# Attention of a layered kernel: turnings of two steps issued together, the value products of both behind them

## What is computed

```python
q = (hidden @ Wq.T).reshape(b, s, 32, 64);  k, v = ...  # 8 heads each, repeated 4 times
q, k = rope(q), rope(k)
logits = jnp.einsum('bhqd,bhkd->bhqk', q, k) / 8
attn = softmax(where(causal, logits, min))
out = jnp.einsum('bhqk,bhkd->bhqd', attn, v).reshape(b, s, 2048) @ Wo.T
x = x + out * silu(sign_layer(xn))
```

## Time and profile before

| | us |
|---|---|
| median of 3 runs | 779.48 (778.21 to 781.17) |
| the profiled execution, its own time | 780.78 |
| its span, first to last instruction | 779.0 |
| TensorE busy, of the span | 706.5 (91%) |
| VectorE, ScalarE, GpSimd busy | 477.7, 417.9, 399.3 |
| share of TensorE in the chain that ended last | 64% |

### The profile page before, as it was taken

How to read it: one execution, slowest core, us unless ns; L and a number is a source line. 1 busy time by engine, 2 the same in 40 slices (tenths; PEclk the granted TensorE clock), 3 DMA queues, 4 the chain that set the end, 5 groups by cost and what they waited for, 6 DMA issues and landing times.

```text
span 779.0 us, 13360 instructions
## 1 busy us (share of the span) xinstructions
PE 706.5 (91%) x4536; PEld 618.6 (79%) x4536; DVE 477.7 (61%) x1023; ACT 417.9 (54%) x1043; POOL 399.3 (51%) x451
## 2 busy tenths in 40 slices
PE   2999999999999991388889999999999999999995
PEld 2887989989989981266678888888888888888874
DVE  7582644423323445485566787777877778777764
ACT  4446244233233234236467776677766777667663
POOL 1412442332332220326777776787767877677460
PEclk9899999999999996599899999999999999999999
DMA  5075877778787505235224323322233222232001
GB/s 187 28 253 186 280 251 249 237 253 254 248 254 250 171 15 155 41 116 147 82 69 117 67 62 69 89 69 64 65 69 89 71 58 67 58 89 56 1 1 54
DMA packets 101859, 96.21 MB, mean 124 GB/s; under 512 B 50592, under 2 KB 72032, under 8 KB 101664
## 3 DMA queue, kind: packets, MB, share of 16 engines
q1 hardware_dynamic: 99584, 89.33, 39.6%
q0 software_dynamic: 2208, 6.03, 2.2%
HBM read 69.24 MB, written 9.31 MB: 101 GB/s over the span
## 4 chain that ended last, share of the span: by engine, by line
PE 64%; DVE 10%; POOL 9%; ACT 8%; issue 6%; SPq 1%; POOLq 1%; DMA 1%; DVEq 0%; ACTq 0%
PE bank L1631 15%; PE bank L1491 8%; PE bank L1665 8%; PE bank L1492 8%; PE bank L1493 8%; PE bank L1487 6%; POOL prob L1449 5%; ACT prob L1264 3%; PE bank L1752 3%; DVE nmax L1010 2%; PE bank L1753 2%; POOL q_lo L1461 2%; ACT kv_hi L1271 2%; DVE o_lo L1023 1%; POOL wq_lo L1429 1%
## 5 line engine op out<-in xcount | busy, mean ns | idle before, releaser
L1449 POOL TENSOR_TENSOR prob<-prob,rinv 128x128 f32<-128x128 f32 (+3 forms) x256 | 177.6, 724 | 102.1 <-DVE rinv L1015 102.1
L1264 ACT ACTIVATE prob<-bank,nmax 128x512 f32<-128x512 f32 (+3 forms) x256 | 133.2, 528 | 45.4 <-DVE nmax L1010 43.9
L1019 DVE TENSOR_TENSOR kv_lo<-bank,kv_hi 128x512 fp32r<-128x512 f32 x160 | 110.0, 687 | 52.7 <-ACT kv_hi L1271 51.8
L1271 ACT ACTIVATE kv_hi<-bank 128x512 fp32r<-128x512 f32 x160 | 96.3, 602 | 78.7 <-PE bank L1487 78.6
L1631 PEld LDWEIGHTS bank<-xgT,wm 128*128 128x128 f32 x920 | 108.1, 192 | 5.3 <-issue 3.8
L1631 PE MATMUL bank<-xgT,wm 128*128 128x128 f32 x920 | 110.3, 275 | 0.5 <-ACT xgT L1173 0.5
L1487 PE MATMUL bank<-cst,prob 128*128 128x128 f32 x640 | 97.8, 276 | 3.0 <-POOL prob L1449 1.2
L1010 DVE TENSOR_REDUCE nmax<-bank 128x1 f32<-128x512 f32 (+2 forms) x192 | 91.1, 502 | 10.8 <-PE bank L1755 10.2
L1491 PE MATMUL bank<-kv_hi,v_lo 128*128 128x128 f32 (+3 forms) x256 | 93.2, 364 | 0.3 <-DVE kv_lo L1019 0.3
L1752 PE MATMUL bank<-kT,qT 128*128 128x512 f32 (+3 forms) x256 | 81.6, 324 | 11.2 <-ACT prob L1264 7.2
L912 DVE TENSOR_TENSOR hE<-sil,bank 128x512 f32<-128x512 f32 x23 | 15.8, 688 | 111.0 <-PE bank L1631 80.5
(11 more groups left out here) (301 smaller groups left out, 1479.0 us busy)
## 6 DMA issues: line engine op xcount, KB each, us to landing
wm<-in_w_moe SPq DMA_DIRECT2D x23, 1280.0 KB
wm<-in_w_moe SPq DMA_DIRECT2D x23, 640.0 KB, 5.7
qT<-q_hi SPq DMA_DIRECT2D x124, 64.0 KB, 2.0
qT<-q_lo SPq DMA_DIRECT2D x124, 64.0 KB, 2.0
k_exp<-k_rows SPq DMA_DIRECT2D x56, 64.0 KB, 2.0
wtl<-in_w_moe_tail SPq DMA_DIRECT2D x46, 64.0 KB
gy<-y_rows SPq DMA_DIRECT2D x8, 256.0 KB, 4.8
wq_raw<-in_w_qkv SPq DMA_DIRECT2D x32, 64.0 KB, 2.5
```

The source lines that it names most:

```text
L1019: TT(p_lo[:, b_, :], bank[2 + b_ % 2][:, :], p_hi[:, b_, :].bitcast(F32), ALU.subtract).then_inc(plo_done, 1)
L1264: ins = actv(prob[:, i % 2, h, POFF[j]:POFF[j] + (j + 1) * P], bk[:, at:at + (j + 1) * P], ACT.Exp, bias=nmax[:, i % 2, h, j:j + 1], accum ...
L1271: actv(p_hi[:, b_, :], bank[2 + b_ % 2][:, :], ACT.Copy).then_inc(phi_done, 1)
L1449: ins = GT(seg, seg, rinv[:, i % 2, k, j:j + 1].to_broadcast([P, (j + 1) * P]), ALU.mult)
```

## The change

The step of T becomes the odd one of the two that it fell into or between: `at = n + 1 - n % 2 + LAG`, which is n + 7 for an even n and n + 6 for an odd one. A follows at + TO_V, and O moves to match. For each pair of steps (n even, n + 1) both T are issued in one odd step, and both A two steps later, behind the next two T. The lists have the same entries as before.

```diff
--- before.py
+++ after.py
@@ -76,10 +76,11 @@
     for r in range(PAIRS):
         for k in range(5):
             n = 5 * r + k
-            own += [(n, 2, "S", r, k), (n, 4, "E", r, k), (n + LAG, 3, "T", r, k), (n + LAG + TO_V, 5, "A", r, k)]
+            at = n + 1 - n % 2 + LAG
+            own += [(n, 2, "S", r, k), (n, 4, "E", r, k), (at, 3, "T", r, k), (at + TO_V, 5, "A", r, k)]
         for h in range(2):
             own += [(5 * r + HEADS_AT[h], 5, "N", r, h)]
-        own += [(5 * r + 4 + LAG + TO_V + 1, 1, "O", r, 0)]
+        own += [(5 * r + 5 - r % 2 + LAG + TO_V + 1, 1, "O", r, 0)]
```

## The result

| | before, us | after, us |
|---|---|---|
| median | 780.3 (778.21 to 781.17, 4 runs) | 789.53 (788.45 to 790.19, 4 runs) |
| ratio of after to before | | 1.0121 [1.0095, 1.0147] |
| the profiled execution: its own time, its span | 780.78, 779.0 | 789.24, 787.4 |
| TensorE busy, granted clock over the span | 706.5, 0.967 | 709.5, 0.966 |
| one middle group, S.0 to S.0 | 48.89 | 49.87 |

The account below looks back on a forecast made before the run. Attention was taken as bound by TensorE's own instructions. Middle groups +3.7 (switches and neighbours included), last group +1.3, tail -0.8 and first group -0.2 summed to +4.0 us, giving 783.5 us; 8-in-10 range 775 to 789.

Parts of the forecast that it names:

- the tail: Behind the wait for the last exponential: three switches saved and the last T ahead of its pair's A, -0.8 us.
- Part 1: TensorE's switches from T to A: half of 160 go, each saving an uncovered weight load of 0.085, -6.8 us.
- walked: Step-by-step timing of a half group of attention on TensorE, ScalarE and VectorE; two halves 49.50 us against 48.91.
- The last group: Last attention group up to the tail: no Q covers the chain, so stalls less the switches cost +1.3 us.
- Part 6: First attention group: small shifts among ScalarE, VectorE and GpSimd, about -0.2 us, bounds -1.5 and +1.5.
- Part 3: ScalarE's paired splits delay exponentials: stalls of 0.90 and 0.50 per half group; six middle groups +3.7 us, switch savings included.
- Part 2: New neighbours of S on TensorE: uncovered loads behind 128-column mask products, 0.06 each, +1.9 us, range 0 to 3.8.
- SP's queue: SP's queue only changes its moments with q_lo, moved by 0.2 us against a need ten steps later: no effect.
- The switch moves and does not go: Rival: each S behind a mask product and each A behind an A pays 0.08; +8.5 us, 788, chance 0.14.
- TensorE stays the bound: Rival: ScalarE's backlog does not form and the stalls go; -7.3 us, 772, chance 0.15.
- exponential.2 before 8.1: Deciding sign for the faster rival: ScalarE's k=2 exponential starting before 8.1 on the walk's scale means no stall.
- stalls at a T: Sign of being wrong: stalls over 0.3 us at a T would mean the turnings' banks, not exponentials, hold TensorE.

Follow-up runs that it names:

- rope_early: The changed kernel with VectorE's second rope pair moved ahead of the two lower splits of its odd step: 785.13 us, ratio 1.0073.
- h_later: The changed kernel with ScalarE's query split (q_hi) moved behind the exponential of the next odd step: 789.69 us, ratio 1.011.
- e_between: The changed kernel with ScalarE's odd-step exponential put between the two upper splits: 804.02 us, ratio 1.0303.
- rope_early_e_between: The changed kernel with the second rope pair ahead of the lower splits and ScalarE's odd-step exponential between the upper splits: 790.05 us, ratio 1.0125.
- rope_early_vo_later: The changed kernel with the second rope pair ahead of the lower splits and the output-weight split moved later, to step 15: 787.35 us, ratio 1.0076.
- a_single: The changed kernel with T still in odd-step pairs but one A in every step, O moved to match: 788.94 us, ratio 1.0118.
- even_pairs: The changed kernel with the pairs one step further, T T A A in even steps and S alone in odd ones: 781.58 us, ratio 1.0012.

## Why the prediction was wrong, point by point

The forecast was no change up to the border of slower (783.5); the kernel is slower, at 789.53, half a microsecond beyond the end of the range. Attention took 6.2 us more than the sum: 2.6 in the middle groups, 2.2 in the first group, 0.9 in the last and 0.5 in the tail.

**Part 1, the switches, -6.8 us: the step that failed.** It took four turnings in 0.36 us for a step of 0.09 each, and the 0.08 too much at the first product for the price of a switch on top. The steps are 0.109, and the last one 0.03, because the first product starts early by the 0.08 that it then takes longer. A switch from T to A therefore costs nothing beyond one turning's step, and halving the number of switches saves nothing. A pair of blocks saves the long first product of its second A and pays the same 0.08 in its eight turnings, 0.80 in place of twice 0.36. 80 pairs at 0.08 are 6.4 us: that much of the booked gain was never there, and it shows wherever TensorE does not wait anyway. One pair by rows: T and A of k = 0 and k = 1 took 1.14 and 1.26 before (501.36 to 502.50, 503.14 to 504.40), 2.40 together, and T T A A of the same shapes 2.38 after (510.65 to 513.03).

The Trainium skill (TensorE: Matmul & The Clock Gate, LDWEIGHTS) gives a load of 128 columns as 128/1.2 = 107 ns, and the 0.109 from turning to turning agrees with it, though each of these loads is shown 0.14 long. Used for each turning of the run, and not for the switch alone, it would have given nearly the right length: seven steps of 0.107 and the short last one make 0.78, an estimate by that page, where 0.79 to 0.80 was measured.

In the middle groups this is the part that shows. The half group is 0.18 longer than walked (24.93 against 24.75). Up to the end of S.1 the ScalarE chain sets the time and the longer turnings are swallowed: S.1 starts 0.10 sooner than walked, its block takes 0.75 (515.35 to 516.10) in place of 0.64 as its first product stands behind a wait, and it ends where the walk had it, 16.24 against 16.23. From there to the next S.4 no S waits, and the walk is missed by two runs of turnings (+0.15) and W (+0.08: it starts behind a 128-column product of A), less 0.05 at S.2, which before stood behind that product. +0.18 in each of 12 half groups is 2.2 of the 2.6 us that the middle groups took beyond the forecast; the rest is the first of them, 50.27. In the tail the start of the last A comes 12.01 us behind its begin, in place of 12.16 (walked: 11.4): the wait of 0.34 is gone, and the three switches brought nothing. The last group took +2.2 in place of +1.3; no run splits that 0.9.

**Part 6, the first group, -0.2 us: +2.0.** It said that the rope pair one lower split later costs 0.2. It forgot who waits for that pair. In this group the sign layer's turnings do, in TensorE's in-order list; timeline of TensorE after, then before:

```profile
399.19 0.66 PE L1488 MATMUL bank<-cst,xn 128*128 128x128 f32 x4 [1.54 <-DVE kv_raw L978]
402.24 1.12 PE L1488 MATMUL bank<-cst,xn 128*128 128x128 f32 x4 [2.40 <-DVE kv_raw L978]
```

```profile
401.74 0.66 PE L1487 MATMUL bank<-cst,xn 128*128 128x128 f32 x4 [1.11 <-DVE kv_raw L977]
404.19 0.66 PE L1487 MATMUL bank<-cst,xn 128*128 128x128 f32 x4 [1.80 <-DVE kv_raw L977]
```

The two waits are 3.94 in place of 2.91. And the second 0.66 has become 1.12: here too the granted clock fell, from 400.1 on, which no part of the prediction has. Windows after, then before:

```profile
400.10:407.00 6.90, 4.76 (x21) 4.58 (x22) 4.20 (x10) 4.10 (x11) 6.00 (x8) 0.51 0.33 97
```

```profile
401.70:408.50 6.80, 4.95 (x37) 4.01 (x37) 5.08 (x10) 4.93 (x15) 6.50 (x8) 1.00 0.30 80
```

At the 1.2 GHz level four blocks (402.24 to 407.28) took 5.04 us; at full clock their like take some 2.8, so the clock cost about 2.2, an estimate from rows of both levels. With the 1.03 of longer waits, less 1.02 that the last wait of the group gives back (0.19 at 412.89 in place of 1.21), that makes 2.2, near the 2.0 measured. rope_early shortens the second wait to 1.14, its clock stayed at 1.00 there, and its group is 1.6 shorter. Over all the kernels the first group took 59.97 to 63.48 in the six where the clock fell at this place (after, h_later, e_between, rope_early_e_between, rope_early_vo_later, a_single) and 55.92 to 59.40 in the eight others, by one profile of each. No run changes the clock alone, with the waits as they are.

**Part 3, ScalarE's queue: right** in its places, with positions within 0.1 over 15 us. TensorE's idle time for the exponential, 13.0 us, stayed under the 15 to 25 that were named (the load queue's is 23.6). What it claims of the cause holds in half: the rope pair ahead of max.1 is on the chain (rope_early), but with one link shortened another takes its place within a few tenths of a microsecond (h_later, rope_early_vo_later).

**Part 2, the neighbours of S, +1.9**, was sized right where it can be seen: behind the 128-column mask product of S.0 the step to W and W's first step take 0.36 together (513.55 to 513.91), where 0.07 and 0.23 make 0.30. That is the 0.06 that it took. The other such place, S.3, is followed by the S.4 that waits anyway. Behind the wider mask products there is no cost, as it said. **SP's queue** stayed without effect.

**The rivals.** "The switch moves and does not go" gave 788 and came nearest, but by another way. Its test was a first product of over 0.47 at an odd S of k = 0; at the S of k = 3 in this half such a product shows 0.52 (520.45), yet the two S together are no longer than before (1.18 from 519.94 to 521.12, where the earlier trace rows give 1.23 for them apart), since it starts that much sooner behind the mask product. What does come back is paid inside the turnings, so that it came near is luck. "TensorE stays the bound" fell with the stalls; its own condition, exponential.2 before 8.1, was missed at 8.94. The test named for being wrong, stalls at a T, did not show in the middle groups. The chances set on "slower", 0.45, were too low for the reason of part 1: of a sum of one gain and several losses, the gain was read at the first product alone, and the step just ahead of it, which takes it back, was not looked at.

**Left open.** Odd pairs cost 9 us and even ones none, and VectorE's rows show the order that differs; but moving the rope pair alone got back only half of it in the groups, and putting the products singly did the same. Which further link of the odd order holds the rest was not isolated; parity moves T, A and O together.

## What to carry to other kernels

Putting like instructions together on the busiest engine also puts the work behind them together on the others, so walk the lists of those engines first, and try the same grouping one step to the side before giving it up: here the parity alone was worth 8 us. On an engine whose instructions overlap, a product that looks long may have started early: before a difference is called a price, look at the step ahead of it, and find a longer run of the same instructions. Look at the clock in the windows of both ends of a stage, and not only in its middle: the waits of 2.50 and 2.17 us at the end of even_pairs were each followed by a stretch at half clock. When several chains end within a few tenths of each other, one edit buys only the distance to the next.

## What the runs showed of the hardware

Turnings of 128 x 128 in fp32 at the full granted clock start 0.109 us apart in most steps, four or eight in a row; the first product behind them starts 0.03 behind the last one and steps 0.08 longer than others of its shape. At the half clock the turnings of a run (404.34 to 405.91 in after) are 0.213 apart. A 384-column product behind a wait for another engine (509.89) takes 0.29 to the next one, where one without a wait (499.86) takes 0.17. The granted clock was at the 1.2 GHz level in after from 400.1 to 407.0, where TensorE had waited 1.54 us (to 399.19) and then 2.40 us (from 399.84, the fall lies in it), and in even_pairs from 748.5 to 751.9 and 765.5 to 768.9, behind waits of 2.50 and 2.17 us; in the kernel before it stayed at 1.00 at the same places, with waits of 1.11 and 1.80, 1.19 and 1.06 us.
